# The tile loop of a feed-forward stage split where its trip count stops being certain

## The reference

```python
router_logits = xt @ gate_w.T
routing_weights = jax.nn.softmax(router_logits.astype(jnp.float32), axis=-1)
top_w, top_idx = jax.lax.top_k(routing_weights, TOP_K)          # 8 of 32
full_w = jnp.zeros_like(routing_weights).at[rows, top_idx].set(top_w)
full_w = full_w / jnp.clip(full_w.sum(axis=-1, keepdims=True), 1e-09, None)
g = jax.nn.silu(jnp.einsum('th,ehi->eti', xt, w_gate))          # h 512, i 192
u = jnp.einsum('th,ehi->eti', xt, w_up)
y = jnp.einsum('eti,eih->eth', g * u, w_down)
out = jnp.einsum('eth,te->th', y, full_w)
```

## Time and profile before

| | us |
|---|---|
| median of 3 runs | 766.03 |
| lowest, highest | 762.21, 766.92 |
| the profiled execution's own time | 762.42 |
| its span | 760.6 |
| TensorE busy (matmuls) | 709.8 (93%) |
| VectorE busy | 567.1 (75%) |
| ScalarE busy | 434.4 (57%) |
| GpSimd busy | 377.1 (50%) |

### The profile page before, as it was taken

The page is one execution under the profiler, slowest core; times in us unless marked ns, Lnnn a source line. Parts: engine busy times, 40 slices in busy tenths (PEclk is TensorE's granted clock), DMA queues, the critical chain, the costliest instruction groups (busy, mean ns, idle before and its releaser), DMA issues.

```text
span 760.6 us, 24425 instructions
## 1 busy us (share of the span) xinstructions
PE 709.8 (93%) x3666; PEld 584.0 (77%) x3667; DVE 567.1 (75%) x1355; ACT 434.4 (57%) x1047; POOL 377.1 (50%) x297
## 2 busy tenths in 40 slices
PE   7999999988688899999999999999999999999993
PEld 5466555656577788889888889889899798899992
DVE  4588888878555587867876878877788678787871
ACT  1775665652034566657566666566666566665662
POOL 2006777767775434444544444434543446344554
PEclk9999999999789999999999999999999999999997
DMA  8997777587898999999999999999999999999996
GB/s 299 352 338 244 280 278 268 216 283 260 300 301 179 184 220 219 229 216 220 220 200 237 226 214 241 216 246 229 230 243 244 224 208 242 241 236 231 208 150 81
DMA packets 174399, 179.78 MB, mean 236 GB/s; under 512 B 36864, under 2 KB 128768, under 8 KB 174368
## 3 DMA queue, kind: packets, MB, share of 16 engines
q0 software_dynamic: 30976, 73.48, 43.1%
q1 hardware_dynamic: 119248, 68.09, 35.3%
q10 hardware_dynamic: 24144, 37.89, 15.1%
HBM read 92.25 MB, written 87.13 MB: 236 GB/s over the span
## 4 chain that ended last, share of the span: by engine, by line
PE 44%; SPq 14%; DMA 12%; issue 12%; POOL 5%; DVE 4%; ACT 3%; ACTq 3%; DVEq 2%; POOLq 0%
SPq L431 9%; PE bank L1485 7%; PE bank L1478 7%; PE bank L1479 7%; DMA x_all<-x_sorted 5%; DMA out_dram<-ctx_all,x_all 5%; POOL x_sorted L488 5%; PE bank L1271 3%; PE bank L1450 3%; SPq L434 2%; PE bank L1451 2%; PE bank L1452 2%; PE bank L1454 2%; PE bank L1453 2%; SPq L414 2%
## 5 line engine op out<-in xcount | busy, mean ns | idle before, releaser
L545 POOL DMA_INDIRECT out_dram<-ctx_all,x_all x144 | 242.8, 1686 | 280.9 <-issue 136.3
L1478 PE MATMUL bank<-gu_hi,xT_hi 128*128 x576 | 196.0, 340 | 3.8 <-DVE gu_lo L1173 3.3
L1479 PE MATMUL bank<-gu_lo,xT_hi 128*128 x576 | 196.2, 341 | 0.0
L761 ACT ACTIVATE ctx_all<-bank 128x512 f32<-128x512 f32 x144 | 85.9, 596 | 101.9 <-issue 85.4
L488 POOL DMA_INDIRECT x_sorted<-xn_kept,slots x96 | 99.3, 1034 | 86.5 <-issue 83.3
L1485 PE MATMUL bank<-gu_hi,xT_lo 128*128 x576 | 137.2, 360 | 0.0
L1157 DVE STREAM_TRANSPOSE x_all<-x_all 128x512 f32<-128x512 f32 x146 | 103.9, 712 | 27.5 <-DMA x_all<-x_sorted 23.4
L1478 PEld LDWEIGHTS bank<-gu_hi,xT_hi 128*128 128x128 f32 x576 | 109.2, 190 | 14.3 <-issue 9.0
L1204 DVE SCALAR_TENSOR_TENSOR probT<-probT,x_all,bank 128x192 f32<-128x192 f32 x144 | 59.5, 413 | 77.8 <-ACT probT L769 67.0
L1479 PEld LDWEIGHTS bank<-gu_lo,xT_hi 128*128 128x128 f32 x576 | 109.1, 189 | 5.4
L748 ACT ACTIVATE xT_hi<-x_all 128x512 fp32r<-128x512 f32 x146 | 91.7, 628 | 32.5 <-DVE x_all L1157 32.0
(11 more groups left out here) (222 smaller groups left out, 1107.4 us busy)
## 6 DMA issues: line engine op xcount, KB each, us to landing
x_all<-x_sorted SPq DMA_DIRECT2D x584, 64.0 KB
gu_raw<-in_w_gate_up_dram ACTq DMA_DIRECT2D x28, 768.0 KB
down_raw<-in_w_down_dram ACTq DMA_DIRECT2D x28, 512.0 KB
x_sorted<-pad_rows SPq DMA_DIRECT2D x1, 8720.0 KB, 30.7
x_all<-in_x_dram SPq DMA_DIRECT2D x8, 512.0 KB, 4.9
ctx_all<-in_ctx_dram SPq DMA_DIRECT2D x8, 512.0 KB, 6.2
out_dram<-x_all SPq DMA_DIRECT2D x8, 512.0 KB
gu_raw<-in_w_gate_up_dram SPq DMA_DIRECT2D x4, 768.0 KB
```

What stands on the lines that cost most here:

```text
L545: pool.indirect_dma_start(out=out, out_offset=bass.IndirectOffsetOnAxis(ap=xw[:, k, E:E + 1].bitcast(I32), axis=0), in_=y_sb[:, i, :], in_ ...
L761: act_e.activation(y_sb[:, i, :], bank[6 + i % 2][:], ACT.Copy).then_inc(S["y_evac"], 1)
L1478: pe.matmul(out_gu, xT_hi[:, s, c * P:(c + 1) * P], gate_up(gu_hi, c), start=(c == 0), stop=False)
L1479: pe.matmul(out_gu, xT_hi[:, s, c * P:(c + 1) * P], gate_up(gu_lo, c), start=False, stop=False)
```

## The change

The loops are cut at quarter 32 (tile 128), up to which every quarter always runs. On TensorE, ScalarE and VectorE there are now three pieces: eight tiles without a loop as before; a loop up to tile 127 with no branch in it (TensorE by eight tiles, the others by four); and a second loop over quarters 32 to 40 with two branches each: below the number of turns it runs four tiles, at the number of turns it runs `end`, which holds the last tiles' pieces. `end` takes its tile number from the loop's own counter, so the second load of the turns and VectorE's operation that wrote `n_turns[1]` are gone. The instructions of a tile, their order, their buffers and their semaphores are the same.

```diff
@@ -270,31 +270,37 @@
-        def run_tiles(eng, step):
+        def run_tiles(eng, step, end):
             turns = load_turns(eng)
             for k in range(SLOTS):
-                step(0, k)
-            with eng.Fori(1, NT // SLOTS) as eight:
-                with eng.If(2 * eight < turns):
+                step(0, 0, k)
+            with eng.Fori(1, LEAST // SLOTS) as eight:
+                for k in range(SLOTS):
+                    step(eight, 0, k)
+            with eng.Fori(LEAST // 4, NT // 4 + 1) as q:
+                with eng.If(q < turns):
                     for k in range(4):
-                        step(eight, k)
-                with eng.If(2 * eight + 1 < turns):
-                    for k in range(4, SLOTS):
-                        step(eight, k)
-            return turns
-
-        def run_quarters(eng, step):
+                        step(0, q, k)
+                with eng.If(q == turns):
+                    end(q)
+
+        def run_quarters(eng, step, end):
             turns = load_turns(eng)
             for k in range(SLOTS):
                 step(k // 4, k % 4)
-            with eng.Fori(2, NT // 4) as q:
+            with eng.Fori(SLOTS // 4, LEAST // 4) as q:
+                for k in range(4):
+                    step(q, k)
+            with eng.Fori(LEAST // 4, NT // 4 + 1) as q:
                 with eng.If(q < turns):
                     for k in range(4):
                         step(q, k)
+                with eng.If(q == turns):
+                    end(q)
...
@@ ScalarE @@
+            def end(turns):
+
+                split_act_hi(4 * turns - 1, 1)
+                evac_y(4 * turns - 2, 2, 16 * turns - 16)
+                evac_y(4 * turns - 1, 3, 16 * turns - 16)
...
-            run_quarters(act_e, ffn)
-
-            last = load_last_turn(act_e)
-            split_act_hi(4 * last + 3, 1)
-            evac_y(4 * last + 2, 2, 16 * last)
-            evac_y(4 * last + 3, 3, 16 * last)
+            run_quarters(act_e, ffn, end)
...
@@ VectorE @@
-            dve.tensor_copy(n_turns[:, 0:1], n_turns_f[:])
-            dve.tensor_scalar(n_turns[:, 1:2], n_turns_f[:], -1.0, None, ALU.add)
+            dve.tensor_copy(n_turns[:], n_turns_f[:])
...
+            def end(turns):
+
+                split_act_lo(4 * turns - 1, 1)
...
-            run_quarters(dve, ffn)
-            split_act_lo(4 * load_last_turn(dve) + 3, 1)
+            run_quarters(dve, ffn, end)
...
@@ TensorE @@
-            def ffn(eight, k):
-                j = SLOTS * eight + k
+            def ffn(eight, q, k):
+                j = SLOTS * eight + 4 * q + k
...
+            def end(turns):
+
+                transpose_act(4 * turns - 1, 1)
+                down(4 * turns - 2, 2, False)
+                down(4 * turns - 1, 3, False)
...
-            run_tiles(pe, ffn)
-            last = load_last_turn(pe)
-            transpose_act(4 * last + 3, 1)
-            down(4 * last + 2, 2, False)
-            down(4 * last + 3, 3, False)
+            run_tiles(pe, ffn, end)
```

More of the change, by code:

```diff
@@ L191, in build @@
         n_tile_b = sb("n_tile_b", [E, 1], BF16)
-        n_turns = sb("n_turns", [1, 2], I32)
+        n_turns = sb("n_turns", [1, 1], I32)
         n_turns_f = sb("n_turns_f", [1, 1])
@@ L309, in tile_is_before, with is_first_of @@
             return type(q) is int and 4 * q + k < first
+        def is_first_of(j, first):
+            return type(j) is int and j < first
         def load_turns(eng):
             return eng.value_load(n_turns[0:1, 0:1], min_val=LEAST // 4, max_val=NT // 4)
-        def load_last_turn(eng):
-            return eng.value_load(n_turns[0:1, 1:2], min_val=LEAST // 4 - 1, max_val=NT // 4 - 1)
         def column_count(k):
@@ L1480, in ffn @@
                 read_next_expert(j, (k + 1) % 4)
-                if not is_before(eight, k, 1):
+                if not is_first_of(j, 1):
                     transpose_act(j - 1, o)
@@ L1486, in ffn @@
                 m.then_inc(S["gu_done"], 1)
-                if not is_before(eight, k, 2):
-                    down(j - 2, (k - 2) % 4, is_before(eight, k, 4))
+                if not is_first_of(j, 2):
+                    down(j - 2, (k - 2) % 4, is_first_of(j, 4))
+            def end(turns):
+                transpose_act(4 * turns - 1, 1)
+                down(4 * turns - 2, 2, False)
+                down(4 * turns - 1, 3, False)
             for to, value in ((experts_reg[0], 1), (half_reg[0], 0)):
                 pe.reg_mov(to, value)
-            run_tiles(pe, ffn)
-            last = load_last_turn(pe)
-            transpose_act(4 * last + 3, 1)
-            down(4 * last + 2, 2, False)
-            down(4 * last + 3, 3, False)
+            run_tiles(pe, ffn, end)
 _INS = ['x', 'ctx_2048', 'L0_xattn_theta_w', 'L0_xattn_theta_b', 'L0_xattn_phi_w', 'L0_xattn_phi_b', 'L0_xattn_g_w', 'L0_xattn_g_b',
```

## The result

| | median us | runs | lowest, highest |
|---|---|---|---|
| before | 766.47 | 4 | 762.21, 767.44 |
| after | 822.33 | 4 | 820.33, 823.31 |

The ratio is 1.078, its 95% interval 1.0745 to 1.0824. The forecast was 764.9 us, within 760.0 and 768.5. The time is far outside, on the side of rival D, and dearer than D was priced.

A forecast was written before the change was run, and what follows sets the result against it. TensorE was taken as fully busy in the loop, the end as set by ScalarE's sequencer and nearly by GpSimd's adds. Tail 0.6 plus branches 0.5 made 1.1 us off the 766.03 us median: 764.9 us, range 760.0 to 768.5.

The forecast's parts named there:

- rival D: Second loop with tail falls out of an instruction store, so jumps fetch: 770.2 us, 766.0 at the low price; chance 0.10.
- packets of the instruction queues in the last 70 us: Sign at the kernel's end that would show the forecast wrong and instruction fetching at work.
- GpSimd's 5.15 us of room: Before tile 139's add, GpSimd waits for earlier adds to land; up to 5.15 us of delay elsewhere would be covered.
- The branches removed: Quarters 2 to 31: 30 compare-and-branches fewer on each of three engines, mostly covered; 0.5 us gain taken.
- the 2.8 us of issue waits: TensorE's waits for its sequencer in the loop, 1.7 us before transposes and 1.1 before down matmuls; upper bound of gain.
- The tail: Last tiles: ScalarE's split of tile 143 2.75 us earlier, near 746.3, its drain 749.3; 0.6 us gain at the end.
- tile 142's add staying at 750.98: GpSimd's own pace holds this add, so tile 143's can come at 752.83, 0.67 us earlier than 753.50.
- rival B: ScalarE's 2.75 us gain at the end comes out whole: 762.8 us, or 760.5 with all issue waits; chance 0.08.
- The sum of 1.1 us in all: Whole kernel: 0.6 us at the end plus 0.5 us from removed branches, off the profiled execution.
- Nothing by the back edges: Quarters 32 to 35: extra back edges and taken branches, 1.7 us on TensorE's and 1.0 on ScalarE's sequencer, cost nothing.
- A: The main forecast for the whole kernel, small gains at the end and from branches: 764.9 us; chance 0.70.
- C: Nothing moves: landing of tile 139's add holds the drain and branches are all covered; 766.0 us, chance 0.12.

The follow-up runs named there:

- before_f1: The kernel before with one semaphore increment nobody waits for ahead of ScalarE's loop; 1059.31 us against 762.31.
- fill_116: The changed kernel with 116 idle increments between ScalarE's two loops; 771.42 us, where the kernel before took 762.31.
- fill_117: fill_116 with one idle increment more between ScalarE's two loops; 823.46 us, where the kernel before took 762.31.
- fill_1: The changed kernel with one idle increment between ScalarE's two loops; 834.92 us, ratio 1.0009 to the kernel before on that chip.
- bound_37: The changed kernel with ScalarE's second loop ended behind the pass that runs the tail; 875.25 us, where the kernel before took 835.33.
- act_only: The changed kernel with old loops and tails on TensorE and VectorE, ScalarE as changed; 901.57 us, where the kernel before took 835.33.
- act_one_f4: The changed kernel with one ScalarE loop over all quarters, tail inside, and four idle increments ahead of it; 761.33 us, ratio 0.9986 to the kernel before.
- act_old: The changed kernel with ScalarE's old loop and tail back, and VectorE's write of n_turns[1]; 835.95 us, ratio 1.0019 to the kernel before.

## Why the prediction was wrong

**The step that failed is the weighing of rival D.** The mechanism was named and its witness too (packets of the instruction queues in the last 70 us). Three things in it were wrong.

*The evidence against it said nothing about the new loop.* "From 345 to 745 us only data queues moved anything" is true and means that the old loop stayed. The text said itself that nothing shows how near the new loop is, and then gave D 0.10. The old loop stood at the very limit: before_f1 shows it for one instruction ahead of it, and by the count one to three ahead or any one more inside would do it. The change adds nine to the loop (the branch over the tail and the tail) and moves it by some 259. Of the 128 places in which a loop of 269 can begin, by the count 116 touch three blocks and 12 touch four (fill_116 and fill_117 show the edge), so 0.10 was, by luck, about the chance of a blind throw. With the edge known, the place could have been counted instead; nothing on record at that time showed the edge.

*The price of a jump was taken from the packets' time.* 0.5 us a packet, 1 to 2 us a jump. The stalls are 2.0 to 5.9 us: a packet's time on the DMA engines is not the time until a sequencer goes on. A pass with nothing in it has three such stalls, 8.4 us from 1017.89 to 1026.27 above (2.12 + 2.97 + 3.10, with 0.19 for the steps). In the first three quarters behind a back edge TensorE lost 11.3, 8.5 and 7.6 us, by the distances of its tiles' first gate matmuls (14.85, then 11.20 and 4.28, then 11.07 us where 3.5 is usual). D had at most 2 us for each and let GpSimd's 5.15 us of room swallow most of them.

*The passes behind the tail were not in the sum at all.* The prediction priced what stands ahead of the last add and took what ScalarE does after it as free. Where nothing is fetched that is right: in fill_1 the four empty passes take 3.1 us and the end comes 7.2 us behind the last add, 7.1 in the kernel before. In the changed kernel they take 35.1 us and put the end 34.2 us behind the last add: 27.1 us of the 61.0. Without them that distance is 6.4 us (bound_37).

With the stalls as they are, D's own sum would have been: the three late quarters 11.3 + 8.5 + 7.6 = 27.4; the tail, from the drain of tile 141 to the last add, 15.5 us (771.85 to 787.36) in place of 8.0, so 7.5; the empty passes 27.1. That is 62.0. Ahead of the tiles the changed kernel lost 2.3 us, and between there and the second loop it gained 3.4; both are left unexplained, two executions can differ by that. With them the sum is 60.9, of 61.0 measured.

**The branches removed.** What comes out was put between nothing and the 2.8 us of issue waits, and 0.5 us was taken. TensorE's issue waits went from 2.8 to 0.8 us, but the other traces don't let the branches be the reason: over its loop act_only, with the old branches on TensorE, has 0.5 us, and act_one_f4, without them, 2.2. Nothing reaches the time either: act_old has TensorE's and VectorE's cut loops at a ratio of 1.0019 [0.9982, 1.0057]. So the term is not to be told from nothing, and what the issue waits are is open.

**The tail.** The split near 746.3 and the drain near 749.3 were right to 0.1 us where nothing is fetched (act_one_f4). The 0.6 us made of them was too small. It rested on tile 142's add staying at 750.98, and that place belongs to an execution in which tile 139's add had come as late as 745.05; in act_one_f4 that add comes at 741.40, and GpSimd then waits for ScalarE again. From the drain of tile 141 to the last add the tail saves 2.4 us in three traces out of three, near the 2.75 us of rival B, which had 0.08. The sum of 1.1 us in all agrees with the ratio of act_one_f4, 0.9986 [0.9962, 1.0009], which is -1.1 us and between -2.9 and +0.7; but so does a saving of 2.4 us, and so does none. It is no proof of the sum, and the version is not shown to beat the kernel before.

**Nothing by the back edges.** "Cost: nothing", as GpSimd has 5.15 us of room. In fill_1 and act_one_f4 nothing speaks against it: from quarter 33 on their TensorE waits 0.6 and 0.5 us for issue (the kernel before not at all). In the changed kernel the room was there too and was smaller than one late quarter.

**The range.** By its own bounds it reaches down to 758.7 us (762.21 - 1.1 - 2.4) and not to 760.0. Nothing hangs on it here, and a range made of A and C had no room for D at these prices anyway.

**The rule that was cited.** The Trainium skill, "Runtime: NRT & Kernel Launch", section Instruction fetch mechanics, warns that a taken branch to outside a small window forces a fetch. The runs agree with the warning, and it deserved more than a sentence. The same section and "Advanced Engine Details and Errata", section ISA Cache, speak of two lines of 256 instructions. The second also says that the line size can be set for each engine. Here the packets on q14 were 8 KB (0.54 MB in 66; the 186 that before_f1 has beyond the kernel before, 1.52 MB, too), and the edge lay at three blocks of 128: with two lines of 256 only one of the two pairs could have an edge. From the start of the old loop (the first loop in fill_116 starts at the same place) to the second loop of fill_116 there are 375 instructions. If the old loop begins at 252 of 256, it ends at 511 and before_f1's reaches 512, a third line; but then fill_116 and fill_117 begin at 115 and 116 and both touch two. If it begins at 124, fill_116 and fill_117 have the edge (511 and 512), and before_f1 at 384 has none. Both pairs showed it, so the measurement decides: on this chip, as it was set, the lines of ScalarE are not two of 256.

## What to carry to other kernels

A loop on an engine's sequencer (here ScalarE's) can cost nothing or some 8 us a pass depending on where its first and last instruction fall, and one idle instruction ahead of it can move it from one to the other. Before a loop is cut, doubled or given a tail, count its instructions and its place on each engine that runs it, register moves of DMA issues included; and where a time changes by far more than the work does, look at the instruction queues' packets before any engine's work. Empty passes behind the last work are part of the program: break off, or make them cheap, where an engine's end can outlast the last transfer.

## What the runs showed of the hardware

ScalarE's sequencer kept a loop that touched three blocks of 128 instructions and fetched in every pass one that touched four, in the twelve loops of the two tables without an exception. The edge was shown by two pairs one instruction apart (p + n - 1 of 383 and 384). In the changed kernel a stall for a fetch took 2.0 to 5.9 us, in its empty passes 2.0 to 3.5, and the last three of these passes had 8.1 to 8.3 us and five packets of 8 KB each (15 packets from 796.5 to 821.1 us).

Why three blocks stay and not four, no run here shows; that the fourth is the one fetched ahead is a guess. The limit was not measured on the other engines. VectorE's second loop has about 170 instructions by count and can't touch four blocks. The other instruction queue, q8, moves packets of 16 KB (0.15 MB in 9) in every kernel; that it is TensorE's is an inference, as its 9 packets never grow with ScalarE's fetching.
